# A gated feed-forward kernel: the value half's bias moved from VectorE into TensorE's PSUM sums, with the gate's, as two 32-row tiles

## The reference

```python
def bit_linear(x, w, b):
    gamma_x = clip(max(abs(x), axis=-1), 1e-05)
    x_dq = clip(round(x * 127 / gamma_x), -128, 127) * gamma_x / 127
    gamma_w = clip(mean(abs(w)), 1e-05)
    w_dq = clip(round(w / gamma_w), -1, 1) * gamma_w
    return x_dq @ w_dq.T + b

gate = silu(bit_linear(x, gate_w, gate_b))
val  = bit_linear(x, val_w, val_b)
out  = bit_linear(gate * val, out_w, out_b)
x    = x + tanh(g_ffn) * out
```

## Time and profile before

| | |
|---|---|
| time, median of 3 runs | 849.53 us (847.89 to 850.29) |
| profiled execution, span from first to last instruction | 846.0 us |
| profiled execution, time of its own | not shown; the runs' median is 3.5 us above its span |
| TensorE matmul busy | 769.7 us, 91% |
| VectorE busy | 699.2 us, 83% |
| ScalarE busy | 534.2 us, 63% |
| GpSimd busy | 240.9 us, 28% |

### The profile page before, as it was taken

The page is one execution under the profiler, slowest core; times in us unless marked ns, Lnnn a source line. Parts: engine busy times, 40 slices in busy tenths (PEclk is TensorE's granted clock), DMA queues, the critical chain, the costliest instruction groups (busy, mean ns, idle before and its releaser), DMA issues.

```text
span 846.0 us, 13511 instructions
## 1 busy us (share of the span) xinstructions
PE 769.7 (91%) x4319; PEld 415.8 (49%) x4374; DVE 699.2 (83%) x1412; ACT 534.2 (63%) x693; POOL 240.9 (28%) x427
## 2 busy tenths in 40 slices
PE   4696688979999999999999999999999999999995
PEld 4442374436545564546444644464445544554442
DVE  6769786997888888888988888888888888779982
ACT  4548858766657655785578457855676556655563
POOL 4101003221342224332423333314421232223421
PEclk9898759999999999999999999999999999999998
DMA  8662435001021103011211121111111020001000
GB/s 273 213 237 74 148 134 171 23 14 38 24 71 37 40 1 93 0 37 37 56 37 37 37 54 39 37 37 43 50 37 37 15 55 26 25 2 51 13 26 25
DMA packets 51660, 50.87 MB, mean 60 GB/s; under 512 B 30876, under 2 KB 30876, under 8 KB 50856
## 3 DMA queue, kind: packets, MB, share of 16 engines
q1 hardware_dynamic: 51624, 50.42, 18.6%
HBM read 39.91 MB, written 10.50 MB: 60 GB/s over the span
## 4 chain that ended last, share of the span: by engine, by line
PE 52%; DVE 25%; issue 11%; ACT 9%; POOL 1%; DMA 1%; DVEq 0%; POOLq 0%; another core or an unknown queue 0%; ACTq 0%
PE psum L1399 16%; PE psum L1444 13%; PE psum L1435 7%; PE psum L1490 6%; ACT arena L749 2%; DVE arena L988 2%; DVE psum L983 2%; PE psum L1427 2%; PE psum L1503 2%; PE psum L1378 1%; PE psum L1402 1%; DVE arena L1077 1%; PE psum L1470 1%; DVE delta L1033 1%; ACT valb_b L656 1%
## 5 line engine op out<-in xcount | busy, mean ns | idle before, releaser
L1399 PE MATMUL psum<-ternary,xqT 128*128 128x512 f16 x1024 | 262.8, 381 | 4.7 <-DVE arena L988 1.5
L554 POOL TENSOR_TENSOR rstd<-var_e,minus_half 128x1 f32<-128x1 f32 x64 | 40.0, 625 | 412.8 <-DVE var_e L1028 262.3
L1399 PEld LDWEIGHTS psum<-ternary,xqT 128*128 128x128 f16 x1024 | 97.3, 99 | 106.7 <-DVE arena L988 3.3
L1435 PE MATMUL psum<-ternary,arena 128*128 128x512 f16 x512 | 128.4, 384 | 1.6 <-ACT arena L726 1.2
L693 ACT ACTIVATE arena<-psum,dequant 128x512 f32<-128x512 f32 x128 | 87.1, 682 | 47.3 <-PE psum L1402 47.0
L983 DVE SCALAR_TENSOR_TENSOR psum<-psum,dequant,valb_b 128x512 f32<-128x512 f32 x128 | 96.2, 752 | 20.2 <-PE psum L1399 19.7
L988 DVE TENSOR_TENSOR arena<-psum,arena 128x512 f32<-128x512 f32 x128 | 88.5, 691 | 20.8 <-ACT arena L693 17.1
L1444 PE MATMUL psum<-wo_hi,arena 128*128 128x512 f16 x256 | 84.4, 392 | 2.1 <-DVE arena L1096 1.5
L1444 PE MATMUL psum<-arena,wq_hi 128*128 128x512 f16 x256 | 77.7, 386 | 6.5 <-ACT arena L740 6.5
L726 ACT ACTIVATE arena<-psum,round_c 128x1024 f16<-128x1024 f16 x64 | 71.3, 1114 | 18.6 <-PE psum L1427 18.3
L701 ACT ACTIVATE arena<-arena,round_c,hscale 128x1024 f32<-128x1024 f32 x64 | 75.9, 1236 | 4.6 <-DVE hscale L1004 4.4
(11 more groups left out here) (181 smaller groups left out, 1352.1 us busy)
## 6 DMA issues: line engine op xcount, KB each, us to landing
arena<-in_x SPq DMA_DIRECT2D x64, 256.0 KB, 2.6
out<-arena SPq DMA_DIRECT2D x32, 256.0 KB, 2.0
arena<-in_L_ffn_gate_w SPq DMA_DIRECT2D x4, 1024.0 KB, 10.6
arena<-in_L_ffn_out_w SPq DMA_DIRECT2D x3, 1024.0 KB, 8.2
ternary<-in_L_ffn_val_w SPq DMA_DIRECT2D x2, 1024.0 KB, 10.4
kcur<-k_scratch SPq DMA_DIRECT2D x64, 32.0 KB, 2.2
ternary<-in_ctx SPq DMA_DIRECT2D x1, 1024.0 KB, 5.3
ternary<-in_L_xattn_Wk SPq DMA_DIRECT2D x1, 1024.0 KB, 8.0
```

The costliest lines, as they stand in the source:

```text
L1399: ins = M.matmul(ps[:], xqT[:, t % 2, k, :], w[:, k, cols], start=(k == 0), stop=(w is wv and k == KC - 1))
L1435: ins = M.matmul(psO[:], hidT[:, k, :], wo2[:, k, :], start=(k == 0), stop=(k == FC - 1))
```

## The change

The value's bias is handled as the gate's is. bias_left, bias_cut, inv, inv_deq, ones_p and bias_dram get a second half for it. Rows 0 to 31 of inv_rows and bias_parts belong to the gate, rows 32 to 63 to the value (GROUP = 32). TensorE makes both bias products first, each over its 32 rows, one into psG and one into psV, and then the four gate and the four value products. VectorE's two instructions become one.

```diff
@@ TensorE, gate_val
-                            pe.wait_ge(s_brow, 16 * PARTS)
-                    for ps, w, done, used in ((psG[i % 2], wg, g_done, silu_done),
-                                              (psV[i % 2], wv, v_done, hid_ready)):
+                            pe.wait_ge(s_brow, 16 * 2 * PARTS)
+                    for g, (ps, used) in enumerate(((psG[i % 2], silu_done), (psV[i % 2], hid_ready))):
                         if n > 2:
                             wait(pe, used, b, n - 2)
+                        rows_g = slice(GROUP * g, GROUP * (g + 1))
+                        M.matmul(ps[:], inv_rows[rows_g, t % 2, :], bias_parts[rows_g, cols], start=True, stop=False)
+                    for ps, w, done in ((psG[i % 2], wg, g_done), (psV[i % 2], wv, v_done)):
                         for k in range(KC):
-                            ins = M.matmul(ps[:], xqT[:, t % 2, k, :], w[:, k, cols], start=(k == 0),
-                                           stop=(w is wv and k == KC - 1))
-                        if w is wg:
-                            ins = M.matmul(ps[:], inv_rows[:, t % 2, :], bias_parts[:, cols],
-                                           start=False, stop=True)
+                            ins = M.matmul(ps[:], xqT[:, t % 2, k, :], w[:, k, cols], start=False,
+                                           stop=(k == KC - 1))
                         ins.then_inc(done.sem, 1)
@@ VectorE, hidden
                     wait(dve, v_done, b, NCH * t + n + 1)
-                    if not prev and (t, n) == (0, 0):
-                        dve.wait_ge(s_vbias, 16)
-                    V.scalar_tensor_tensor(out=psV[n % 2], in0=psV[n % 2], scalar=dequant[:, t, 1:2],
-                                           in1=valb_b[:, n * CW:(n + 1) * CW],
-                                           op0=ALU.mult, op1=ALU.add).then_inc(vb_ready.sem, 1)
-                    wait(dve, vb_ready, b, NCH * t + n + 1)
                     wait(dve, silu_done, b, NCH * t + n + 1)
-                    V.tensor_tensor(part, psV[n % 2], part, ALU.mult).then_inc(hid_ready.sem, 1)
+                    V.scalar_tensor_tensor(out=part, in0=psV[n % 2], scalar=dequant[:, t, 1:2], in1=part,
+                                           op0=ALU.mult, op1=ALU.mult).then_inc(hid_ready.sem, 1)
@@ GpSimd, update_rest
-                whole, left = inv[:, 0:1], inv[:, 1:2]
-                G.tensor_scalar(whole, inv_deq[:], xr[:, t:t + 1], None, ALU.mult).then_inc(iv_ready.sem, 1)
+                whole, left = (inv[:, n, :].rearrange("p (g a) -> p g a", a=1) for n in range(2))
+                cols = inv_cols[:, t % 2, :].rearrange("p (g c) -> p g c", c=GROUP)
+                G.tensor_scalar(inv[:, 0, :], inv_deq[:], xr[:, t:t + 1], None, ALU.mult).then_inc(iv_ready.sem, 1)
...
-                    G.tensor_tensor(inv_cols[:, t % 2, j:PARTS * PARTS:PARTS], ones_p[:],
-                                    src.to_broadcast([P, PARTS]), ALU.mult).then_inc(iv_part.sem, 1)
+                    G.tensor_tensor(cols[:, 0:2, j:PARTS * PARTS:PARTS], ones_p[:].rearrange("p (g c) -> p g c", g=2),
+                                    src.to_broadcast([P, 2, PARTS]), ALU.mult).then_inc(iv_part.sem, 1)
...
-                        G.tensor_tensor(left, src, inv_cols[:, t % 2, j:j + 1], ALU.subtract).then_inc(iv_left.sem, 1)
+                        G.tensor_tensor(left, src, cols[:, 0:2, j:j + 1], ALU.subtract).then_inc(iv_left.sem, 1)
@@ SP, set-up
-                        sp.wait_ge(s_wabs, 3 * W_CHUNKS - 1)
-                        sp.dma_start(valb_b[:, :], bcast(val_b, F)).then_inc(s_vbias, 16)
...
-            sp.dma_start(bias_left[:, :], gate_b.rearrange("(p c) -> p c", p=P)).then_inc(s_bias, 16)
+            for g, bias in enumerate((gate_b, val_b)):
+                sp.dma_start(bias_left[:, g, :], bias.rearrange("(p c) -> p c", p=P)).then_inc(s_bias, 16)
...
-            for i in range(PARTS):
-                sp.dma_start(bias_parts[PARTS * i:PARTS * (i + 1), :],
-                             bias_dram[i:i + 1, :].to_broadcast([PARTS, F])).then_inc(s_brow, 16)
+            for g in range(2):
+                for i in range(PARTS):
+                    row = GROUP * g + PARTS * i
+                    sp.dma_start(bias_parts[row:row + PARTS, :],
+                                 bias_dram[g, i:i + 1, :].to_broadcast([PARTS, F])).then_inc(s_brow, 16)
@@ memory
-        valb_b = sb("valb_b", [P, F])
-        unused_abs = valb_b[:, 0:F // 2].bitcast(F16)
+        unused_abs = sb("unused_abs", [P, F], F16)[:, :]
```

More of the change, by code:

```diff
@@ L93, in build @@
         k_dram = nc.dram_tensor("k_scratch", [P, 2 * KC, B, T], F16, kind="Internal").ap()
-        bias_dram = nc.dram_tensor("bias_scratch", [PARTS, F], BF16, kind="Internal").ap()
+        bias_dram = nc.dram_tensor("bias_scratch", [2, PARTS, F], BF16, kind="Internal").ap()
         v_dram = nc.dram_tensor("v_scratch", [BT, D], F32, kind="Internal").ap()
@@ L158, in build @@
         bias_parts = sb("bias_parts", [P, F], BF16)
-        bias_left = sb("bias_left", [P, FC])
-        bias_cut = sb("bias_cut", [P, PARTS, FC], BF16)
-        valb_b = sb("valb_b", [P, F])
-        unused_abs = valb_b[:, 0:F // 2].bitcast(F16)
+        bias_left = sb("bias_left", [P, 2, FC])
+        bias_cut = sb("bias_cut", [P, 2, PARTS, FC], BF16)
+        unused_abs = sb("unused_abs", [P, F], F16)[:, :]
         unused_abs_last = room(11)[:, 2 * D:].bitcast(F16)
@@ L166, in build @@
         inv_rows = sb("inv_rows", [P, 2, P], BF16)
-        inv = sb("inv", [P, 2])
-        inv_deq = sb("inv_deq", [P, 1])
-        ones_p = sb("ones_p", [P, PARTS])
+        inv = sb("inv", [P, 2, 2])
+        inv_deq = sb("inv_deq", [P, 2])
+        ones_p = sb("ones_p", [P, 2 * PARTS])
         eye_b16 = sb("eye_b16", [P, P], BF16)
@@ L252, in build @@
         s_bias0, s_bias = sem("bias_space_zeroed"), sem("biases_loaded")
-        s_vbias = sem("val_bias_loaded")
         s_bol, s_bst, s_brow = sem("bo_loaded"), sem("bias_parts_stored"), sem("bias_rows_loaded")
@@ L330, in build @@
         silu_done = per_row("silu_done", NT * NCH)
-        vb_ready = per_row("val_biased", NT * NCH)
         hid_ready = per_row("hidden_ready", NT * NCH)
@@ L499, in _ @@
             sp.wait_ge(s_bpart, PARTS)
-            sp.dma_start(bias_dram.rearrange("j (p c) -> p j c", p=P), bias_cut[:, :, :]).then_inc(s_bst, 16)
+            for g in range(2):
+                sp.dma_start(bias_dram[g].rearrange("j (p c) -> p j c", p=P), bias_cut[:, g, :, :]).then_inc(s_bst, 16)
             for t in range(2):
                 normed_x(1, t)
-            sp.wait_ge(s_bst, 16)
-            for i in range(PARTS):
-                sp.dma_start(bias_parts[PARTS * i:PARTS * (i + 1), :],
-                             bias_dram[i:i + 1, :].to_broadcast([PARTS, F])).then_inc(s_brow, 16)
+            sp.wait_ge(s_bst, 16 * 2)
+            for g in range(2):
+                for i in range(PARTS):
+                    row = GROUP * g + PARTS * i
+                    sp.dma_start(bias_parts[row:row + PARTS, :],
+                                 bias_dram[g, i:i + 1, :].to_broadcast([PARTS, F])).then_inc(s_brow, 16)
             sp.wait_ge(s_kv, 1)
@@ L611, in bias_to_parts @@
             def bias_to_parts():
-                pool.wait_ge(s_bias, 16)
+                pool.wait_ge(s_bias, 16 * 2)
                 for i in range(PARTS):
@@ L615, in bias_to_parts @@
                         pool.wait_ge(s_bleft, i)
-                    G.tensor_copy(bias_cut[:, i, :], bias_left[:]).then_inc(s_bpart, 1)
+                    G.tensor_copy(bias_cut[:, :, i, :], bias_left[:]).then_inc(s_bpart, 1)
                     if i < PARTS - 1:
                         pool.wait_ge(s_bpart, i + 1)
-                        G.tensor_tensor(bias_left[:], bias_left[:], bias_cut[:, i, :],
+                        G.tensor_tensor(bias_left[:], bias_left[:], bias_cut[:, :, i, :],
                                         ALU.subtract).then_inc(s_bleft, 1)
@@ L903, in weight_scale @@
                 V.reciprocal(wrec[:, n:n + 1], wmean[:, n:n + 1]).then_inc(s_wrec, 1)
-                if n == 0:
+                if n < 2:
                     dve.wait_ge(s_wrec, n + 1)
-                    V.tensor_scalar(inv_deq[:], wrec[:, n:n + 1], QMAX, None, ALU.mult)
+                    V.tensor_scalar(inv_deq[:, n:n + 1], wrec[:, n:n + 1], QMAX, None, ALU.mult)
                 then(V.tensor_scalar(deq[:, n:n + 1], wmean[:, n:n + 1], 1.0 / QMAX, None, ALU.mult))
```

## The result

| | before | after |
|---|---|---|
| time, median (lowest to highest) of 4 runs | 849.58 us (847.89 to 850.29) | 859.12 us (857.75 to 859.71) |
| profiled execution, span | 846.0 us | 857.1 us |
| TensorE, VectorE, ScalarE, GpSimd busy | 769.7, 699.2, 534.2, 240.9 us | 793.2, 626.0, 537.8, 242.7 us |

What follows compares the result with a forecast made beforehand. TensorE was taken as the bound, busy 86.60 of a steady row's 88.91 us. The 846.0 us span, plus 21.1 for the pair, minus 8.9 of VectorE's relief, plus 3.5 from span to median, gave 861.7 us; range 841 to 884.

Steps and rivals of the forecast that it cites:

- The pair: Two 32-row bias products per block on TensorE: side by side, about one 0.165 us gap lost, 21.1 us in all.
- The free pair: Rival, chance 0.35: the bias products run side by side, shape changes cost almost nothing, 3.8 us; total 844.4 us.
- no overlap: Rival, chance 0.15: the two 32-row bias products run one behind the other, 0.216 us each, 27.6 us; total 868.2.
- two full gaps of 0.165: Rival, chance 0.12: both shape changes in each block expose the whole 0.165 us, 42.2 us; total 882.8 us.
- VectorE's relief: TensorE's stalls behind VectorE's later results give back 9.9 us, 8.9 less the moved wait; bounds 0 and 13.
- the moved wait: Gate products now also wait for the value bank: 0.15 us more in each of seven tiles, 1.0 us lost.
- enough for both: In the tile shown, VectorE's result 0.73 us earlier removes TensorE's stalls at 413.12 (0.48) and 413.84 (0.32).
- No block's instruction lies between: The 0.76 us stall before the attention products at 378.58 isn't recovered: VectorE waits there for ScalarE, behind the exponentials.
- a mean of two cases: The 0.165 us per pair was taken as the mean of no gap (0) and two gaps (0.33) per block.
- The steady row: A steady row of the batch should last 90.8 us; 88.2 would mean free pair, 91.7 no overlap, 93.5 two gaps.
- VectorE's busy time: VectorE loses one of two instructions in each of 128 blocks, 93 us of 699, leaving near 606 us busy.
- The rest at nothing: GpSimd's wider scale split, doubled bias loads, the dropped broadcast and ScalarE's own buffer: no net cost, bounds -1 to +1.

Runs made afterwards that it cites:

- e2_gate32: The kernel before, with only its one gate bias product cut to rows 0 to 31, no product added: 866.06 us, ratio 1.0196.
- e3_relief: The kernel before, with VectorE's one instruction and the value's bias left out of the computation, TensorE unchanged: 838.23 us, ratio 0.9877.
- the tall form: The changed kernel with both bias products zero-padded to 128 rows: 863.63 us; with the value's product behind the gate's four again: 860.52 us.

## Why the prediction was right, and where its sizes were off

861.7 us was forecast and 859.1 measured. The direction and its cause held: the extra TensorE time is more than VectorE gives back. Two terms were off, in opposite directions, and a third rests on a misread row.

- **The pair.** Forecast 0.165 us a block, 21.1 us, as "side by side, with about one such gap lost over both changes", 0.165 being what the shown end hides. Measured are two gaps of 0.10, 0.197 a block, 25.2 us: 4.1 too little. The 0.165 was not the right unit. Each change loses about 0.10 whether it follows a product of 512 columns, a transpose or a float32 product, so the loss is a constant of the change and not the rest of the product in front. The free pair fell by e2_gate32, "no overlap" by the 0.003 us, two full gaps of 0.165 by the table of distances.
- **VectorE's relief.** Forecast 9.9 us less 1.0 for the moved wait (its own point below). Alone it is 11.1 us (e3_relief), inside the bounds of 0 and 13. The working took idle time only from shown ends; a stall behind a matmul also holds its hidden 0.165, so 0.48 us in the profile was 0.64 in starts. That VectorE's earlier result would be "enough for both" stalls of the tile fell: alone it removes the 0.64, but the second, GpSimd's, goes only from 0.49 to 0.41, and ScalarE's grows from 0.16 to 0.38. "No block's instruction lies between" held in its substance: the stall before the attention products stayed with TensorE unchanged, at 0.65 for 0.76 us. In the changed kernel it is 0.43 to 0.46:

```profile
382.72 1.97 PE L1483 MATMUL psum<-vcur,arena 128*128 128x66 f32 x16 [0.43 <-DVE delta L1027]
```

- **What the sum left out.** TensorE's own extra time fills stalls. If VectorE and ScalarE, not TensorE, set when a result comes, then a TensorE that is later by its gaps waits less for it. With whatever the moved wait costs taken off, this is 4.3 us (the difference of the other terms, not a measurement of its own), and the forecast simply added the two terms. With it, 849.3 + 25.2 - 11.1 - 4.3 = 859.1. So the relief and the filling together were 6.5 us larger than the 8.9 forecast, the pair 4.1 larger than its 21.1, and the errors mostly cancelled: that the total came within 2.6 us is in good part luck, and the 0.165 itself was, by the prediction's own words, a mean of two cases that no row decided between. The steady row shows the same: 90.8 forecast, 90.39 measured.
- **The moved wait.** Forecast 1.0 us from a misread row: "0.41 lost" at 409.28 was 0.19 and the slot of the bias product that is missing from the trace. By the same working the wait would then have cost 0.56 - 0.19 = 0.37 us a tile, 2.6 in all. Measured in the changed kernel it is 0.02 us in each of six rows, since TensorE reaches the fourth block just as VectorE is done. In the tall form the order is worth about 1 us, through ScalarE; whether the packed form loses that too wasn't tried, and the filling above is counted with it taken off.
- **VectorE's busy time.** Forecast near 606 us, measured 626.0. The one instruction takes 746 ns, as forecast (752). But line 1036 went from 824 to 1064 ns in 32 instructions, 7.6 us more, and two other lines by 2.3 together; the groups' sum fell by 81 us, the busy time by 73. Line 1036 uses rstd, which GpSimd makes, so its shown time may hold some waiting, now that VectorE gets there earlier; that was not tested, nor was the rest traced. In e3_relief, where the relief stands alone, the line is as long (1099 ns), so it comes with the relief.
- **The rest at nothing.** GpSimd's split takes 235 ns for 6 columns against 230 for 3, and line 1406 has no stall.

## What to carry to other kernels

Where TensorE is full, a small product is not cheap because it is small: each trip from the full-height shape to another and back cost 0.2 us here, so a padded full-height product (0.216 us) was almost as good as a packed pair (0.197), and far better than a single 32-row product (0.216 + 0.197). Keep tiles of one shape together, or pad. And before moving work from VectorE to a full TensorE, find the few instructions for whose lateness TensorE waits: relieving 128 blocks cost 1.2%, relieving only the one block in front of that wait in each of seven rows gained 0.5%.

## What was not expected of the hardware

- A change of tile shape costs 0.093 to 0.103 us each way with 32-row and 64-row tiles (0.115 on the way back behind four tiles of 64 columns; for float32 the way in was measured, 0.093), and the next weights aren't loaded under the product in front: behind a product of 512 columns the load starts 0.307 us after that product's start, where otherwise it starts 0.002 after.
- Four products of 32 rows by 64 columns, in four places of the array, start within 0.01 us and take the slot of one.
- A product of 32 rows takes its 512 columns no faster than one of 128: both are shown at 0.38 us, a modelled length, and the next product starts 0.317 us behind the small one, not less than the pitch of 0.216.
- A matmul whose record is missing from a trace can pass for a stall. The weight loads show it: 0.41 us "lost" was 0.19.
